# Curvature flow on one core: one clip for both curvatures, K added a period later, and GpSimd's second sum behind the addition of H

## The chip, the cores and the metric

The kernel runs on one core of a Trainium2 chip. The metric is the device time of one execution in microseconds, lower is better. Engines are named as in the profile: PE is TensorE, DVE is VectorE, ACT is ScalarE, POOL is GpSimd, SP is SyncE, which here only issues DMAs.

## What is computed

The input is 8 x 16 images of 512 x 512 floats. The first layer is ten steps of a curvature flow on each image, the second a pair of 3 x 3 convolutions over 16 channels with a residual. Per step (`_derivs` gives Sobel derivatives, each clipped to 10):

```python
ux, uy, uxx, uxy, uyy = _derivs(u)
g2 = ux * ux + uy * uy
denK = jnp.maximum(1.0 + g2, EPS)
K = jnp.clip((uxx * uyy - uxy * uxy) / (denK * denK + EPS), -5.0, 5.0)
denH = jnp.sqrt(1.0 + g2 + EPS)
H = ((1.0 + uy * uy) * uxx - 2.0 * ux * uy * uxy + (1.0 + ux * ux) * uyy) / (2.0 * denH ** 3 + EPS)
H = jnp.clip(H, -5.0, 5.0)
diff = jnp.clip(alpha * K + beta * H, -1.0, 1.0)
u = u + DT * diff
# then the border rows and columns are copied from their neighbours
```

After ten steps the layer gives `0.7 * u + 0.3 * x`; the convolutions follow.

## The kernel before

A short first stage scans the input and picks one of two versions of the flow. Here it picks the tame one (tiles named `tame_`), in which no field clip is needed and K and H are added to U directly. The last stage holds the two convolutions and is not touched.

The flow holds four images on the chip at once, U as 128 partitions x 2048 per image, worked on in halves ("chunks") of 128 x 1024. Every step of a chunk is one period of a software pipeline; 32 rounds x 10 steps x 8 chunks are 2560 periods. In period k each engine executes a fixed list, written out by hand in its own `period` function, which mixes chunk k with chunks k - 1 to k - 4. Engines wait for each other by semaphores, one per kind of operation, that count up by 2 for each chunk; `done(t, c)` is the count after chunk c. Since chunks k and k - 2 share buffers (`c % 2`), an operation on chunk k that writes a buffer waits for the last reader of chunk k - 2.

- PE (L646, L656): the derivatives `ux`, `uy` of chunk k (eight matmuls each), then for chunk k - 1 the subtraction of uxy squared from `ps["uxx"]` with a negative unit matrix, then `uyy`, `uxy`, `uxx` of k. `ux` waits for `term_uyy` of k - 1, `uy` for `term_uxy` of k - 1 (they share PSUM slots), `uyy` for `square_ux` and `uxy` for `square_uy` of k, `uxx` for `curvature_k` of k - 1.
- DVE: for k - 1 `term_uxx`, `term_uxy` (L517, into uy2 and cross), `determinant` (L540); for k - 2 `add_h` (L517, U from ux2); for k `multiply_first` (L536); in some periods `blend` (L517 into stage), the final 0.7/0.3 mix of a finished image; for k - 1 `curvature_k` (L559); for k `sum_squares` (L517 into slope); for k - 1 `curvature_h` (L570), `clip_k` (L565), `clip_h` (L575), `add_k` (L517, U from uyy); for k `term_uyy` (L517 into ux2).
- ACT: `power` (L441), `log_power` (L446) of k - 1, `copy_ux` (L397) of k, `inverse_k` (L436) of k - 1, `square_ux` (L402), `square_uy` (L408) of k, `inverse_h` (L452, into PSUM) of k - 1, `square_slope` (L426), `copy_uyy` (L414) of k, `high` (L391) of k - 4, `square_uxy` (L420) and `logs` (L431, both halves of slope) of k. In blend periods `scale` (L457) as well.
- POOL: `second_terms` (L362) and `numerator_h` (L368) of k - 1, both sums into ux2, then `low` (L356) of k - 4, the low part of U's split in two rounded parts.
- SP: the exchange of split halos (L281) in two halves, around `edge_columns` (L290), which waits for `updated`, and `edge_rows` (L298, L300).

`sum_squares` waits for `square_uy`, which waits for `multiply_first`. `curvature_h` waits for `numerator_h` and `inverse_h`. `high` waits for the border rows of its chunk, `low` for `high`. K lies in `uyy[c % 2]` and H in `ux2[c % 2]`, both in SBUF, as are U, slope, cross and stage; the derivatives and `inverse` lie in PSUM. The operations `blend` and `scale` occur in 8 periods of every round, 256 in all.

## Time and profile before

| | us |
|---|---|
| median of 3 runs | 38702.86 |
| the runs | 38694.59 to 38705.76 |
| the profiled execution | 38698.44 |
| its span | 38696.7 |
| DVE busy | 34434.0 |
| PE busy | 34434.2 |
| ACT busy | 33167.9 |
| POOL busy | 20465.8 |

The flow fills the span from about 412 to 35005 us; the scan is ahead of it, the convolutions behind. A busy time is the union of an engine's instructions. Instructions of one engine overlap a little in the records: the next starts slightly before the one ahead is noted as ended, so the distance from start to start is what an instruction costs its engine. "L517" is one helper line for all `scalar_tensor_tensor` operations; the tiles tell them apart.

### The profile page before, as it was taken

To read this page: it belongs to the slowest core of one execution; us is meant where nothing else is said; L and a number is where in the kernel's file an instruction comes from. 1 tells how busy PE (TensorE), PEld (TensorE's weight loads), DVE (VectorE), ACT (ScalarE), POOL (GpSimd) and SP (SyncE) were. 2 spreads that over 40 slices of the span, in tenths; PEclk is the share of its full clock that TensorE was granted. 3 is DMA by queue.
4 is the path that set the end of the run, shared out by engine and by line. 5 is a ranking of instruction groups with operands and counts; after the bars stand their busy time and mean duration, and the time that the engine had idled before them with its cause. 6 is when DMAs were issued, how large, how long until landed. Compare 5 with 4: busy or idle time off the path is not lost. (4 is left out here: it accounts for less than half of the span.)

```text
span 38696.7 us, 453600 instructions
## 1 busy us (share of the span) xinstructions
PE 34434.2 (89%) x126400; PEld 23294.9 (60%) x126400; DVE 34434.0 (89%) x33108; ACT 33167.9 (86%) x33722; POOL 20465.8 (53%) x7685
## 2 busy tenths in 40 slices
PE   5888888888888888888888888888888888889999
PEld 3666666666666666666666666666666666666666
DVE  8999999999999999999999999999999999993111
ACT  5999999999999999999999999999999999994333
POOL 3555555555555556555555555555555555550000
PEclk9999999999999999999999999999999999999999
DMA  5333333333333333333333333333333333333333
GB/s 189 83 83 82 82 75 78 83 83 82 82 83 83 82 79 74 81 83 83 83 82 83 83 83 76 77 81 83 83 83 82 83 83 80 73 82 83 87 87 85
DMA packets 2687511, 3261.71 MB, mean 84 GB/s; under 512 B 2266180, under 2 KB 2266308, under 8 KB 2364740
## 3 DMA queue, kind: packets, MB, share of 16 engines
q1 hardware_dynamic: 2686276, 3247.70, 33.5%
q8 instruction: 475, 7.78, 0.1%
q14 instruction: 760, 6.23, 0.0%
HBM read 582.33 MB, written 268.44 MB: 22 GB/s over the span
## 5 line engine op out<-in xcount | busy, mean ns | idle before, releaser
L646 PE MATMUL tame_slot<-tame_split,tame_M 128*128 128x512 f32 x51200 | 15156.1, 418 | 4131.5 <-DVE tame_ux L517 3386.6
L646 PEld LDWEIGHTS tame_slot<-tame_split,tame_M 128*128 128x128 f32 x51200 | 9160.8, 190 | 10140.8 <-issue 2690.5
L646 PE MATMUL tame_slot<-tame_halo,tame_M 128*128 128x512 f32 x51200 | 14319.2, 402 | 0.0
L356 POOL TENSOR_TENSOR tame_split<-tame_U,tame_split 128x1024 fp32r<-128x1024 f32 x2560 | 6232.0, 2434 | 12755.0 <-ACT tame_split L391 12755.0
L646 PEld LDWEIGHTS tame_slot<-tame_halo,tame_M 128*128 128x128 f32 x51200 | 9757.9, 191 | 2513.8
L368 POOL TENSOR_TENSOR tame_ux<-tame_ux,tame_cross 128x1024 f32<-128x1024 f32 x2560 | 8071.5, 3153 | 433.4 <-POOL tame_ux L362 433.4
L362 POOL TENSOR_TENSOR tame_ux<-tame_ux,tame_uy 128x1024 f32<-128x1024 f32 x2560 | 6161.8, 2407 | 972.6 <-DVE tame_uy L517 972.6
L431 ACT ACTIVATE tame_slope<-tame_slope 128x2048 f32<-128x2048 f32 x2560 | 4895.4, 1912 | 0.0
L656 PE MATMUL tame_slot<-tame_uxy,tame_unit 128*128 128x512 f32 x10240 | 4810.6, 592 | 5.4 <-DVE tame_slot L540 5.4
L426 ACT ACTIVATE tame_slope<-tame_slope 128x1024 f32<-128x1024 f32 x2560 | 2716.8, 1061 | 2141.4 <-issue 2139.4
L559 DVE TENSOR_TENSOR tame_uyy<-tame_slot,tame_slope 128x1024 f32<-128x1024 f32 x2560 | 3132.2, 1223 | 945.6 <-PE tame_slot L656 938.1
L517 DVE SCALAR_TENSOR_TENSOR tame_U<-tame_ux,tame_par,tame_U 128x1024 f32<-128x1024 f32 x2560 | 3694.1, 1443 | 0.1
L517 DVE SCALAR_TENSOR_TENSOR tame_U<-tame_uyy,tame_par,tame_U 128x1024 f32<-128x1024 f32 x2560 | 3272.3, 1278 | 0.0
L536 DVE TENSOR_TENSOR tame_cross<-tame_cross,tame_slot 128x1024 f32<-128x1024 f32 x2560 | 3093.9, 1209 | 158.5 <-PE tame_slot L646 157.2
L517 DVE SCALAR_TENSOR_TENSOR tame_uy<-tame_uy,tame_slot 128x1024 f32<-128x1024 f32 x2560 | 3106.9, 1214 | 27.0 <-issue 27.0
L540 DVE TENSOR_TENSOR tame_slot<-tame_uyy,tame_slot 128x1024 f32<-128x1024 f32 x2560 | 3127.3, 1222 | 0.0
L517 DVE SCALAR_TENSOR_TENSOR tame_slope<-tame_ux,tame_uy 128x1024 f32<-128x1024 f32 x2560 | 3110.9, 1215 | 1.8 <-ACT tame_uy L408 1.3
L517 DVE SCALAR_TENSOR_TENSOR tame_ux<-tame_ux,tame_slot 128x1024 f32<-128x1024 f32 x2560 | 3106.6, 1214 | 2.2 <-ACT tame_uyy L414 2.2
L570 DVE TENSOR_TENSOR tame_ux<-tame_ux,tame_slot 128x1024 f32<-128x1024 f32 x2560 | 3108.1, 1214 | 0.0
L517 DVE SCALAR_TENSOR_TENSOR tame_cross<-tame_cross,tame_slot 128x1024 f32<-128x1024 f32 x2560 | 3107.2, 1214 | 0.0
L862 DVE SCALAR_TENSOR_TENSOR res<-po,vec,xin 96x512 f32<-96x512 f32 x672 | 501.9, 747 | 2838.7 <-PE po L883 2838.7
L441 ACT ACTIVATE tame_slope<-tame_slope 128x1024 f32<-128x1024 f32 x2560 | 2718.2, 1062 | 234.9
(74 smaller groups left out, 38207.5 us busy)
## 6 DMA issues: line engine op xcount, KB each, us to landing
tame_halo<-tame_split SPq DMA_DIRECT2D x2560, 520.0 KB
tame_halo<-tame_split SPq DMA_DIRECT2D x2560, 260.0 KB
tame_halo<-tame_split SPq DMA_DIRECT2D x5120, 65.0 KB
tame_U<-in_x SPq DMA_DIRECT2D x256, 512.0 KB, 3.9
tame_stage<-in_x SPq DMA_DIRECT2D x128, 1024.0 KB, 4.9
mixed<-tame_stage SPq DMA_DIRECT2D x128, 1024.0 KB, 6.4
out<-res SPq DMA_DIRECT2D x672, 192.0 KB
xin<-mixed SPq DMA_DIRECT2D x344, 256.0 KB, 4.6
```

Source lines behind the costliest of these rows:

```text
L356: nc.gpsimd.tensor_tensor(split_rows(c, 1), half_rows(c), split_rows(c, 0).bitcast(F32), ALU.subtract).then_inc(lo_ready, 2)
L362: nc.gpsimd.tensor_tensor(ux2[c % 2][:, :], ux2[c % 2][:, :], uy2[c % 2][:, :], ALU.add).then_inc(sum_h, 2)
L368: nc.gpsimd.tensor_tensor(ux2[c % 2][:, :], ux2[c % 2][:, :], cross[c % 2][:, :], ALU.add).then_inc(num_h_ready, 2)
L431: nc.scalar.activation(both, both, ACT.Ln, bias=EPS).then_inc(logs_ready, 2)
L441: nc.scalar.activation(s, s, ACT.Exp, scale=1.5, bias=math.log(2.0)).then_inc(power_ready, 2)
L517: return nc.vector.scalar_tensor_tensor(out=out, in0=a, scalar=s, in1=b, op0=op0, op1=op1)
L536: nc.vector.tensor_tensor(cross[c % 2][:, :], cross[c % 2][:, :], ps["uy"][:, :], ALU.mult).then_inc(cross_ready, 2)
L540: nc.vector.tensor_tensor(ps["uxx"][:, :], uyy[c % 2][:, :], ps["uxx"][:, :], ALU.mult).then_inc(prod_k, 2)
L559: nc.vector.tensor_tensor(uyy[c % 2][:, :], ps["uxx"][:, :], slope[c % 2][:, 1, :], ALU.mult).then_inc(k_ready, 2)
L570: nc.vector.tensor_tensor(ux2[c % 2][:, :], ux2[c % 2][:, :], inverse[:, :], ALU.mult).then_inc(h_ready, 2)
L646: last = nc.tensor.matmul(ps[name][:, b * BANK:(b + 1) * BANK], M[0:lanes, matrix, :], rows(c, part)[:, b * y:(b + 1) * y, :], start=(n < ...
L656: last = nc.tensor.matmul(ps["uxx"][:, b * BANK:(b + 1) * BANK], unit[:, 0, :], uxy2[:, b * BANK:(b + 1) * BANK], start=False, stop=True, ...
```

## The change

K and H of a chunk now both lie in `slope[c % 2]`, K in half 1 and H in half 0, and a single instruction over both halves (128 x 2048), `clip_both`, takes the place of `clip_k` and `clip_h`. `add_k` moves from the end of the period of chunk k - 1 to just ahead of `add_h`, one period later. `uyy` becomes a single tile, and the waits on reuse follow the new owners of the buffers. `numerator_h` on GpSimd also waits for `updated` of the chunk before it, that is for `add_h` in the same period. ACT's order changes: `square_ux` behind `copy_ux`, then `inverse_k`, `inverse_h`, `scale`, `high`, then `square_uy`, `copy_uyy`, `square_slope`, `square_uxy`, `logs`.

```diff
--- before.py
+++ after.py
@@ -148,7 +148,8 @@
         def pair(name):
             return [sb(f"{name}{j}", [P, HALF]) for j in range(2)]
 
-        ux2, uy2, cross, uyy = pair("ux2"), pair("uy2"), pair("cross"), pair("uyy")
+        ux2, uy2, cross = pair("ux2"), pair("uy2"), pair("cross")
+        uyy = sb("uyy", [P, HALF])
         slope = [sb(f"slope{j}", [P, 2, HALF]) for j in range(2)]
         uxy2 = sb("uxy2", [P, HALF])
         par = sb("par", [P, 4])
@@ -194,9 +195,8 @@
         sum_h = sem("sum_h")
         num_h_ready = sem("num_h_ready")
         k_ready = sem("k_ready")
-        k_clipped = sem("k_clipped")
+        both_clipped = sem("both_clipped")
         h_ready = sem("h_ready")
-        h_clipped = sem("h_clipped")
         k_added = sem("k_added")
         diff_sum = sem("diff_sum")
         diff_clipped = sem("diff_clipped")
@@ -362,16 +362,18 @@
                 nc.gpsimd.tensor_tensor(ux2[c % 2][:, :], ux2[c % 2][:, :], uy2[c % 2][:, :],
                                         ALU.add).then_inc(sum_h, 2)
 
-            def numerator_h(t, c):
+            def numerator_h(t, c, after_update):
                 pool.wait_ge(cross_term, done(t, c))
                 pool.wait_ge(sum_h, done(t, c))
+                if after_update:
+                    pool.wait_ge(updated, done(t, c - 1))
                 nc.gpsimd.tensor_tensor(ux2[c % 2][:, :], ux2[c % 2][:, :], cross[c % 2][:, :],
                                         ALU.add).then_inc(num_h_ready, 2)
 
             def period(t, k, kind, r):
                 if exists(kind, k - 1):
                     second_terms(t, k - 1)
-                    numerator_h(t, k - 1)
+                    numerator_h(t, k - 1, exists(kind, k - 2))
                 if exists(kind, k - 4) and goes_on(kind, k - 4):
                     low(t, k - 4)
 
@@ -398,7 +400,7 @@
 
             def square_ux(t, c, fresh):
                 if not fresh:
-                    act.wait_ge(updated, done(t, c - 2))
+                    act.wait_ge(h_ready, done(t, c - 2))
                 nc.scalar.activation(ux2[c % 2][:, :], ps["ux"][:, :], ACT.Square).then_inc(ux2_ready, 2)
 
             def square_uy(t, c, fresh):
@@ -407,11 +409,11 @@
                     act.wait_ge(sum_h, done(t, c - 2))
                 nc.scalar.activation(uy2[c % 2][:, :], ps["uy"][:, :], ACT.Square).then_inc(uy2_ready, 2)
 
-            def copy_uyy(t, c, fresh):
+            def copy_uyy(t, c, first):
                 act.wait_ge(ready["uyy"], done(t, c))
-                if not fresh:
-                    act.wait_ge(k_added, done(t, c - 2))
-                nc.scalar.activation(uyy[c % 2][:, :], ps["uyy"][:, :], ACT.Copy).then_inc(uyy_copied, 2)
+                if not first:
+                    act.wait_ge(prod_k, done(t, c - 1))
+                nc.scalar.activation(uyy[:, :], ps["uyy"][:, :], ACT.Copy).then_inc(uyy_copied, 2)
 
             def square_uxy(t, c, first):
                 act.wait_ge(ready["uxy"], done(t, c))
@@ -422,7 +424,7 @@
             def square_slope(t, c, fresh):
                 act.wait_ge(slope_ready, done(t, c))
                 if not fresh:
-                    act.wait_ge(k_ready, done(t, c - 2))
+                    act.wait_ge(k_added, done(t, c - 2))
                 nc.scalar.activation(slope[c % 2][:, 1, :], slope[c % 2][:, 0, :], ACT.Square).then_inc(slope2_ready, 2)
 
             def logs(t, c):
@@ -471,21 +473,18 @@
                     log_power(t, k - 1)
                 if exists(kind, k):
                     copy_ux(t, k, fresh)
+                    square_ux(t, k, fresh)
+                if exists(kind, k - 1):
+                    inverse_k(t, k - 1)
+                    inverse_h(t, k - 1, kind == "first" and k == 1)
                 if exists(kind, k - 3) and ends(kind, k - 3):
                     scale(r, k - 3)
-                if exists(kind, k - 1):
-                    inverse_k(t, k - 1)
-                if exists(kind, k):
-                    square_ux(t, k, fresh)
-                    square_uy(t, k, fresh)
-                if exists(kind, k - 1):
-                    inverse_h(t, k - 1, kind == "first" and k == 1)
-                if exists(kind, k):
-                    square_slope(t, k, fresh)
-                    copy_uyy(t, k, fresh)
                 if exists(kind, k - 4) and goes_on(kind, k - 4):
                     next_high(t, k - 4, kind, r)
                 if exists(kind, k):
+                    square_uy(t, k, fresh)
+                    copy_uyy(t, k, first)
+                    square_slope(t, k, fresh)
                     square_uxy(t, k, first)
                     logs(t, k)
 
@@ -526,7 +525,7 @@
                 dve.wait_ge(ux2_ready, done(t, c))
                 dve.wait_ge(uy2_ready, done(t, c))
                 if not fresh:
-                    dve.wait_ge(inv_h_ready, done(t, c - 2))
+                    dve.wait_ge(updated, done(t, c - 2))
                 stt(slope[c % 2][:, 0, :], ux2[c % 2][:, :], 1.0, uy2[c % 2][:, :], ALU.add,
                     ALU.add).then_inc(slope_ready, 2)
 
@@ -537,7 +536,7 @@
                                         ALU.mult).then_inc(cross_ready, 2)
 
             def determinant(t, c):
-                nc.vector.tensor_tensor(ps["uxx"][:, :], uyy[c % 2][:, :], ps["uxx"][:, :], ALU.mult).then_inc(prod_k, 2)
+                nc.vector.tensor_tensor(ps["uxx"][:, :], uyy[:, :], ps["uxx"][:, :], ALU.mult).then_inc(prod_k, 2)
 
             def term_uyy(t, c):
                 dve.wait_ge(uyy_copied, done(t, c))
@@ -556,35 +555,32 @@
             def curvature_k(t, c):
                 dve.wait_ge(num_k_ready, done(t, c))
                 dve.wait_ge(inv_k_ready, done(t, c))
-                nc.vector.tensor_tensor(uyy[c % 2][:, :], ps["uxx"][:, :], slope[c % 2][:, 1, :],
-                                        ALU.mult).then_inc(k_ready, 2)
-
-            def clip_k(t, c):
-                K = uyy[c % 2][:, :]
-                dve.wait_ge(k_ready, done(t, c))
-                nc.vector.tensor_scalar(K, K, CURVATURE_CLIP, -CURVATURE_CLIP, ALU.min, ALU.max).then_inc(k_clipped, 2)
+                K = slope[c % 2][:, 1, :]
+                nc.vector.tensor_tensor(K, ps["uxx"][:, :], K, ALU.mult).then_inc(k_ready, 2)
 
             def curvature_h(t, c):
                 dve.wait_ge(num_h_ready, done(t, c))
                 dve.wait_ge(inv_h_ready, done(t, c))
-                nc.vector.tensor_tensor(ux2[c % 2][:, :], ux2[c % 2][:, :], inverse[:, :], ALU.mult).then_inc(h_ready, 2)
-
-            def clip_h(t, c):
-                Hh = ux2[c % 2][:, :]
+                nc.vector.tensor_tensor(slope[c % 2][:, 0, :], ux2[c % 2][:, :], inverse[:, :], ALU.mult).then_inc(
+                    h_ready, 2)
+
+            def clip_both(t, c):
+                both = slope[c % 2][:, :, :]
+                dve.wait_ge(k_ready, done(t, c))
                 dve.wait_ge(h_ready, done(t, c))
-                nc.vector.tensor_scalar(Hh, Hh, CURVATURE_CLIP, -CURVATURE_CLIP, ALU.min, ALU.max).then_inc(h_clipped, 2)
+                nc.vector.tensor_scalar(both, both, CURVATURE_CLIP, -CURVATURE_CLIP, ALU.min, ALU.max).then_inc(
+                    both_clipped, 2)
 
             def add_k(t, c):
-                K = uyy[c % 2][:, :]
-                dve.wait_ge(k_clipped, done(t, c))
+                K = slope[c % 2][:, 1, :]
+                dve.wait_ge(both_clipped, done(t, c))
                 if tame:
                     stt(half(c), K, a_dt, half(c), ALU.mult, ALU.add).then_inc(k_added, 2)
                 else:
                     nc.vector.tensor_scalar(K, K, a_dt, None, ALU.mult).then_inc(k_added, 2)
 
             def add_h(t, c):
-                K, Hh = uyy[c % 2][:, :], ux2[c % 2][:, :]
-                dve.wait_ge(h_clipped, done(t, c))
+                K, Hh = slope[c % 2][:, 1, :], slope[c % 2][:, 0, :]
                 dve.wait_ge(k_added, done(t, c))
                 if tame:
                     stt(half(c), Hh, b_dt, half(c), ALU.mult, ALU.add).then_inc(updated, 2)
@@ -607,6 +603,7 @@
                     term_uxy(t, k - 1)
                     determinant(t, k - 1)
                 if exists(kind, k - 2):
+                    add_k(t, k - 2)
                     add_h(t, k - 2)
                 if exists(kind, k):
                     clip("ux", t, k)
@@ -620,9 +617,7 @@
                     sum_squares(t, k, kind == "first" and k < 2)
                 if exists(kind, k - 1):
                     curvature_h(t, k - 1)
-                    clip_k(t, k - 1)
-                    clip_h(t, k - 1)
-                    add_k(t, k - 1)
+                    clip_both(t, k - 1)
                 if exists(kind, k):
                     clip("uyy", t, k)
                     term_uyy(t, k)
```

## Rows read from the trace of the kernel before

**Rows 1.** The page, part 1: busy time of each engine, its share, instructions.

```profile
PE 34434.2 (89%) x126400; PEld 23294.9 (60%) x126400; DVE 34434.0 (89%) x33108; ACT 33167.9 (86%) x33722; POOL 20465.8 (53%) x7685
```

**Rows 2.** Timeline, VectorE, a steady period: start, duration, engine, line, out<-in [idle before].

```profile
5011.40 1.22 DVE L517 SCALAR_TENSOR_TENSOR tame_uy<-tame_uy,tame_slot 128x1024 f32<-128x1024 f32 x1
5012.53 1.22 DVE L517 SCALAR_TENSOR_TENSOR tame_cross<-tame_cross,tame_slot 128x1024 f32<-128x1024 f32 x1
...
5014.80 1.44 DVE L517 SCALAR_TENSOR_TENSOR tame_U<-tame_ux,tame_par,tame_U 128x1024 f32<-128x1024 f32 x1
5016.16 1.21 DVE L536 TENSOR_TENSOR tame_cross<-tame_cross,tame_slot 128x1024 f32<-128x1024 f32 x1
5017.77 1.23 DVE L559 TENSOR_TENSOR tame_uyy<-tame_slot,tame_slope 128x1024 f32<-128x1024 f32 x1 [0.40 <-PE tame_slot L656]
5018.91 1.22 DVE L517 SCALAR_TENSOR_TENSOR tame_slope<-tame_ux,tame_uy 128x1024 f32<-128x1024 f32 x1
5020.05 1.22 DVE L570 TENSOR_TENSOR tame_ux<-tame_ux,tame_slot 128x1024 f32<-128x1024 f32 x1
...
5021.78 0.69 DVE L575 TENSOR_SCALAR tame_ux<-tame_ux 128x1024 f32<-128x1024 f32 x1
5022.38 1.28 DVE L517 SCALAR_TENSOR_TENSOR tame_U<-tame_uyy,tame_par,tame_U 128x1024 f32<-128x1024 f32 x1
5023.58 1.21 DVE L517 SCALAR_TENSOR_TENSOR tame_ux<-tame_ux,tame_slot 128x1024 f32<-128x1024 f32 x1
5024.71 1.22 DVE L517 SCALAR_TENSOR_TENSOR tame_uy<-tame_uy,tame_slot 128x1024 f32<-128x1024 f32 x1
```

**Rows 3.** Timeline, ScalarE, the same period and the next.

```profile
5010.63 1.92 ACT L431 ACTIVATE tame_slope<-tame_slope 128x2048 f32<-128x2048 f32 x1
5012.64 1.06 ACT L441 ACTIVATE tame_slope<-tame_slope 128x1024 f32<-128x1024 f32 x1
...
5020.21 1.06 ACT L426 ACTIVATE tame_slope<-tame_slope 128x1024 f32<-128x1024 f32 x1 [0.75 <-issue]
...
5030.81 1.03 ACT L408 ACTIVATE tame_uy<-tame_slot 128x1024 f32<-128x1024 f32 x1
```

**Rows 4.** Instructions on U: duration min/median/max in ns, first and last start, form.

```profile
L356 POOL TENSOR_TENSOR tame_split<-tame_U,tame_split x2560: 2167/2438/2460, 388.8 to 34924.8; 128x1024 fp32r<-128x1024 f32 x197
L517 DVE SCALAR_TENSOR_TENSOR tame_U<-tame_uyy,tame_par,tame_U x2560: 1269/1278/1284, 433.1 to 34997.8; 128x1024 f32<-128x1024 f32 x197
L517 DVE SCALAR_TENSOR_TENSOR tame_U<-tame_ux,tame_par,tame_U x2560: 1285/1444/1457, 438.8 to 34999.2; 128x1024 f32<-128x1024 f32 x197
...
L517 DVE SCALAR_TENSOR_TENSOR tame_stage<-tame_U,tame_stage x256: 1216/2249/3361, 1413.4 to 35004.8; 128x1024 f32<-128x1024 f32 x128
```

**Rows 5.** Timeline, GpSimd, the same steady period.

```profile
5012.75 2.40 POOL L362 TENSOR_TENSOR tame_ux<-tame_ux,tame_uy 128x1024 f32<-128x1024 f32 x1 [0.34 <-DVE tame_uy L517]
5015.32 3.15 POOL L368 TENSOR_TENSOR tame_ux<-tame_ux,tame_cross 128x1024 f32<-128x1024 f32 x1 [0.17 <-POOL tame_ux L362]
```

**Rows 6.** Timeline, GpSimd, the program's first period.

```profile
425.92 2.38 POOL L368 TENSOR_TENSOR tame_ux<-tame_ux,tame_cross 128x1024 f32<-128x1024 f32 x1 [0.17 <-POOL tame_ux L362]
```

**Rows 7.** Timeline, all engines, two periods with a blend (L517 into tame_stage).

```profile
1476.96 1.21 DVE L517 SCALAR_TENSOR_TENSOR tame_slope<-tame_ux,tame_uy 128x1024 f32<-128x1024 f32 x1
...
1486.67 3.14 POOL L368 TENSOR_TENSOR tame_ux<-tame_ux,tame_cross 128x1024 f32<-128x1024 f32 x1 [0.17 <-POOL tame_ux L362]
...
1488.64 2.25 DVE L517 SCALAR_TENSOR_TENSOR tame_stage<-tame_U,tame_stage 128x1024 f32<-128x1024 f32 x1
...
1491.95 1.21 DVE L517 SCALAR_TENSOR_TENSOR tame_slope<-tame_ux,tame_uy 128x1024 f32<-128x1024 f32 x1
...
1497.88 1.83 PE L646 MATMUL tame_slot<-tame_split,tame_M 128*128 128x512 f32 x4 [1.95 <-DVE tame_ux L517]
```

**Rows 8.** Timeline, TensorE, the steady period: second derivative, then the subtraction.

```profile
5013.81 1.22 PE L646 MATMUL tame_slot<-tame_split,tame_M 128*128 128x512 f32 x4
...
5015.80 1.88 PE L656 MATMUL tame_slot<-tame_uxy,tame_unit 128*128 128x512 f32 x4
```

## The prediction

> **What bounds the kernel now.** I read the page's first part, then a timeline of one steady period, engine by engine, then durations by tile, then a stretch with the blend. The page has PE and DVE both busy 89% of the span and ACT 86% [rows 1]; none is plainly the bound, so the period must be walked. On DVE (DVE names VectorE, ACT ScalarE, PE TensorE, POOL GpSimd) the period runs from `term_uxx` at 5011.40 to the next at 5024.71: 13.31 us [rows 2]. A tensor operation with two inputs holds its place for 1.13 to 1.14 us, a clip for 0.60, `add_k` for 1.20, and `add_h` for 1.36. There is one idle gap, before `curvature_k`, ended by PE's subtraction (0.40 noted; the start comes 1.61 after `multiply_first` where 1.13 would do, so 0.48). Without it DVE's work is 12.83.
>
> ACT is nearly as tight. From `sum_squares` (5018.91) to `square_slope` is 1.30, from there to the next `square_uy` 10.60 with no gap, its 1.03 and a signal of 0.11 (between the 0.09 from PE to `curvature_k` and the 0.13 from DVE to POOL [rows 2, 5, 8]) release the next `sum_squares`: 13.04 around [rows 2, 3]. So no rearrangement that keeps this loop wins more than 0.27 us a period.
>
> The rows of most weight are those where DVE and POOL meet. `add_h` (inputs U and the H tile, both in SBUF) takes 1.44, but 1.285 at its shortest [rows 4]; it starts 0.35 before `second_terms` ends on POOL, and loses 0.16 [rows 2, 5]. POOL's `numerator_h`, started 0.92 before `add_h` ends, takes 3.15; in the very first period, with no `add_h` beside it, 2.38 [rows 5, 6]: it loses 0.77. The blend, again two SBUF inputs, starts at 1488.64 under a POOL operation that ends at 1489.81, and takes 2.25 in place of 1.22; the longest blend took 3.36 [rows 4, 7]. If it streams for its last 1.22 us, it got going 0.14 before POOL ended. Meanwhile `multiply_first` and `curvature_k`, with one PSUM input, take their 1.21 and 1.23 under the same POOL operation [rows 2, 5]. I read this as: a DVE operation that needs both of its SBUF inputs and a POOL operation take turns, whole instruction by whole instruction, first come first.
>
> **The change, part by part.** There are 2560 periods (one for every `add_k` [rows 4]); 256 hold a blend, 2304 don't. I set zero at the start of `sum_squares` in the new order.
>
> *Clips.* Two of 0.60 become one over 2048 elements. A pitch of 0.60 is 0.07 besides 0.53 for 1024 elements (two-input operations: 0.07 and 1.07), so the double one is 1.14: gain 0.06. But it now directly follows `curvature_h`, on which it waits, where `clip_k` stood between. A dependent operation can't start 0.08 before the end of the one ahead, as DVE's others do. ACT's `power` shows a dependent start 0.09 after the end (5010.63 + 1.92 to 5012.64, [rows 3]). For DVE I take 0.06, between 0 and 0.10: `curvature_h` holds its place for 1.28 instead of 1.13. Cost 0.15 (0.08 to 0.19).
>
> *`add_k` moved.* It comes right in front of `add_h`, which waits for it: again 0.15 (0.08 to 0.19). And it falls where `add_h` falls today: 3.40 after `term_uxx`, while `second_terms` on POOL, started 1.35 after `term_uxx`, runs to 3.75 [rows 2, 5]. So it pays the 0.16 that `add_h` pays: 1.50 in all.
>
> *The wait on POOL.* `numerator_h` starts only once `add_h` has ended, so neither blocks the other: `add_h` holds 1.20, and POOL's operation takes 2.38. Gain for DVE 0.16. Who waits for it: `curvature_h`, later by four DVE operations, and `low` queued behind it on POOL; see below.
>
> *DVE's sum, nothing yet in its way:* `sum_squares` 1.13, `curvature_h` 1.28, `clip_both` 1.14, `term_uyy` 1.13, `term_uxx` 1.13, `term_uxy` 1.14, `determinant` 1.13, `add_k` 1.50, `add_h` 1.20, `multiply_first` 1.13, `curvature_k` 1.13: 13.04.
>
> *PE.* The unit subtraction begins 1.99 after `uy` begins and takes 1.88; `curvature_k` starts 3.96 after `uy`'s start, which follows `term_uxy`'s start by 1.28 [rows 2, 8]: 5.24. Today only 4.76 of DVE work lies between, hence the gap of 0.48. The new order has `add_k` in there as well: 1.14 + 1.13 + 1.50 + 1.20 + 1.13 = 6.10. The gap vanishes.
>
> *ACT reordered.* `square_ux` and `high` come earlier, `copy_uyy` now follows `square_uy`. The same operations stand between `square_slope` and `square_uy`, save that `inverse_h` replaces `copy_uyy`: 13.04 within 0.05. But `multiply_first` now comes late: start to end 1.21, signal 0.10, `square_uy` 1.03, signal 0.11: `sum_squares` follows it by 2.45, DVE's own order by 2.26. That is 0.19 of new waiting: 13.23. The new conditions on `slope`, `ux2` and the single `uyy` tile name operations half a period old or more; I cost them at nothing. The SP queue keeps its order: `edge_columns` waits for `updated`, which comes 2.4 ahead of `sum_squares` (2.67 now), and the first half of the exchange can start earlier, as `low` does.
>
> *`low`, the expensive part.* `add_h` ends at -2.37 (0.08 after `multiply_first` starts). POOL begins `numerator_h` 0.13 later (as 5012.62 to 5012.75 [rows 2, 5]) and ends at +0.14. `high` has been done since about -1.0, so `low` starts at once. `sum_squares`, two SBUF inputs, already runs since 0; `low` waits until it ends at 1.22. As a POOL operation then needs what `numerator_h` needed after `add_h`, its base (2.17 for `low` [rows 4]) less about 0.15, `low` ends near 3.24. `clip_both` wants to start at 2.41. If it takes turns with POOL too, it gets going 0.14 before that end, at 3.10: 0.69 lost. No POOL operation meets a clip today, so the bounds are 0 and 2.17. I take the 0.69, since the nearest rows speak for it: a clip does 1024 elements in 0.69 where others need 1.22 [rows 2], two at a time, SBUF to SBUF, so it needs as much of SBUF as a two-input operation.
>
> The Trainium skill says the same of both kinds: "GPSIMD Engine Reference", section "Key points", has contention with DVE instructions in a 2-port perf mode or with two SBUF inputs. Of the second kind [rows 4 to 7] agree; of the first no row here shows anything. By this rule the loss is the 0.69, without it the sum would stay at 13.23.
>
> Period: 13.23 + 0.69 = 13.92; I round to 13.88, as 0.14 may be 0.19 by `add_h`'s own row (5015.15 less 5014.96). Against 13.31: +0.57 x 2304 = +1313.
>
> *Blend periods.* Today 14.99 from `sum_squares` to `sum_squares` [rows 7]. New: the blend follows `multiply_first` while POOL runs `numerator_h`; it gets going 0.14 before that ends, at 2.37 after `add_h`'s end, and ends at 3.59. `low` waits for it and ends at 3.59 + 2.02 = 5.61. `sum_squares` could start at 4.64 but gets going at 5.47, in place of 2.37; `clip_both` is then free (less 0.69). 13.92 + 3.10 - 0.69 = 16.33, +1.3 x 256 = +333. PE then idles longer ahead of `ux` than the 1.95 after which a half derivative took 1.83 instead of 1.22 [rows 7, 8], the granted clock at the lower of its levels; up to 1.4 a period, at most 360, only in the range.
>
> Sum: +1646 on the profiled execution's 38698.4 (its span of 38696.7 and 1.7 around it; 4 under the median of the runs, 38702.9): 40,344.
>
> **Rivals.**
> A. *The clip doesn't take turns with POOL.* For: no row shows that it does. Against: its speed. Steady period 13.19, -0.12 x 2304 = -276, blend +333: +57, 38,760. Chance 0.11.
> B. *Faster: `low` is out of the clip's way*, because POOL isn't held by `sum_squares` when it comes second, or finishes before 2.41. `low` would run from 0.14 to 2.3, and the blend periods cost what they cost now. This decides if `low` ends under 2.41. With short signals the period falls toward the 13.04 of ACT's loop: -0.12 to -0.27, centre -0.2 x 2560 = -510: 38,190. Against: `numerator_h` was held 0.77 by `add_h` in just this way. Chance 0.15.
> C. *`low` gets in ahead of `sum_squares`.* It starts 0.14 behind it, so a signal or two decides. Then `sum_squares` loses some 2.0 and the clip nothing: 13.23 + 2.0 = 15.2, +1.9 x 2304 + 333 = +4700: 43,400. Against: the order of starts holds itself up, both hang on `add_h`. Chance 0.05.
> D. *Dependent DVE starts cost nothing.* "VectorE: DVE Perf Modes", section "The DRAIN you can't avoid", has a semaphore between copies cost nothing extra. By that the two terms of 0.15 go: -0.30 x 2560 = -768. As a mechanism of this kernel, priced from rows: DVE operations start 0.08 before the end of the one ahead [rows 2], and a dependent one would too; 40,344 - 768 = 39,580. ACT's 0.09 after the end speaks against it. Chance 0.07.
>
> **How the numbers follow.** Forecast 0.62, own range 39,900 to 40,750; A 0.11, B 0.15, C 0.05, D 0.07. The range from 38,500 to 40,800 leaves out C and most of B. Under 0.2% (77 us) a measurement tells nothing from no change. Slower: forecast, C, D and a fourth of A, 0.77; same: most of A, 0.08; faster: B, 0.15.
>
> **What would show it.** Right: one clip of 128x2048, over 1.7 on average against 1.2 uncontended; `low` near 3.0 instead of 2.44; `numerator_h` near 2.4; `add_k` 1.44 and `add_h` 1.28; no idle before `curvature_k` by PE; `sum_squares` idle about 0.2 behind ACT. Wrong: a clip of 1.2 with `low` beside it (A); `low` at 2.2 to 2.4 (B); `sum_squares` over 3 (C); the start of `add_h` before the end of `add_k` (D); a clip of 2.2 with nothing beside it, which would mean one element at a time and near +1.1 a period without my 0.69.

## The result and the profile after

The changed kernel takes 41,177.5 us (median of 4 runs, 41,160.7 to 41,304.3) against 38,698.7 before: a ratio of 1.065, with a 95% interval of 1.063 to 1.067. (A ratio is a kernel's time over that of the kernel before; its interval stands behind it.) It is slower, as forecast, but by 2479 us where 1646 were forecast, and outside the range. The profiled execution took 41,304.3 (span 41,302.5), the longest of the four, 2606 over the one of before.

The page of the changed kernel, part 1 and three groups of part 5 (busy us, mean ns | idle before, releaser); the first row answers to [rows 1]:

```profile
PE 34840.2 (84%) x126400; PEld 23669.3 (57%) x126400; DVE 36722.5 (89%) x30548; ACT 33735.5 (82%) x33722; POOL 20031.4 (48%) x7685
...
L370 POOL TENSOR_TENSOR tame_ux<-tame_ux,tame_cross 128x1024 f32<-128x1024 f32 x2560 | 6143.0, 2400 | 6779.9 <-DVE tame_U L516 6779.7
L356 POOL TENSOR_TENSOR tame_split<-tame_U,tame_split 128x1024 fp32r<-128x1024 f32 x2560 | 7849.8, 3066 | 142.7 <-ACT tame_split L393 140.8
...
L571 DVE TENSOR_SCALAR tame_slope<-tame_slope 128x2048 f32<-128x2048 f32 x2560 | 4492.4, 1755 | 346.5
```

DVE is busier by 2289 us with fewer instructions; `numerator_h` (L370) fell to its 2.4, `low` (L356) rose from 2.43 to 3.07, and the one clip (L571) takes 1.76 on average where the two took 1.37 together.

A steady period, all engines, in order of time; it answers to [rows 2, 3, 5]:

```profile
2015.07 1.23 DVE L516 SCALAR_TENSOR_TENSOR tame_slope<-tame_ux,tame_uy 128x1024 f32<-128x1024 f32 x1 [0.18 <-ACT tame_uy L410]
2015.16 3.23 POOL L356 TENSOR_TENSOR tame_split<-tame_U,tame_split 128x1024 fp32r<-128x1024 f32 x1
...
2016.21 1.21 DVE L564 TENSOR_TENSOR tame_slope<-tame_ux,tame_slot 128x1024 f32<-128x1024 f32 x1
...
2017.56 1.90 DVE L571 TENSOR_SCALAR tame_slope<-tame_slope 128x2048 f32<-128x2048 f32 x1
...
2019.38 1.21 DVE L516 SCALAR_TENSOR_TENSOR tame_ux<-tame_ux,tame_slot 128x1024 f32<-128x1024 f32 x1
...
2020.51 1.21 DVE L516 SCALAR_TENSOR_TENSOR tame_uy<-tame_uy,tame_slot 128x1024 f32<-128x1024 f32 x1
...
2021.86 2.40 POOL L362 TENSOR_TENSOR tame_ux<-tame_ux,tame_uy 128x1024 f32<-128x1024 f32 x1 [3.47 <-DVE tame_uy L516]
2022.78 1.22 DVE L539 TENSOR_TENSOR tame_slot<-tame_uyy,tame_slot 128x1024 f32<-128x1024 f32 x1
...
2023.91 2.83 DVE L516 SCALAR_TENSOR_TENSOR tame_U<-tame_slope,tame_par,tame_U 128x1024 f32<-128x1024 f32 x2
...
2026.65 1.21 DVE L535 TENSOR_TENSOR tame_cross<-tame_cross,tame_slot 128x1024 f32<-128x1024 f32 x1
...
2026.88 2.41 POOL L370 TENSOR_TENSOR tame_ux<-tame_ux,tame_cross 128x1024 f32<-128x1024 f32 x1 [2.63 <-DVE tame_U L516]
...
2027.79 1.22 DVE L559 TENSOR_TENSOR tame_slope<-tame_slot,tame_slope 128x1024 f32<-128x1024 f32 x1
2027.95 1.03 ACT L410 ACTIVATE tame_uy<-tame_slot 128x1024 f32<-128x1024 f32 x1
...
2029.18 1.23 DVE L516 SCALAR_TENSOR_TENSOR tame_slope<-tame_ux,tame_uy 128x1024 f32<-128x1024 f32 x1 [0.18 <-ACT tame_uy L410]
```

From `sum_squares` to `sum_squares` it is 14.11. `low` starts 0.09 behind `sum_squares` and takes 3.23; the clip starts 2.49 after `sum_squares` and takes 1.90. `numerator_h` starts 0.23 after `multiply_first` does and is done in 2.41, `add_k` and `add_h` together take 2.83, and there is no gap ahead of `curvature_k` now.

Minimum, median and maximum of two operations on slope, in ns:

```profile
L516 DVE SCALAR_TENSOR_TENSOR tame_slope<-tame_ux,tame_uy x2560: 1206/1225/3292, 419.3 to 37586.9; 128x1024 f32<-128x1024 f32 x197
...
L571 DVE TENSOR_SCALAR tame_slope<-tame_slope x2560: 1226/1891/1910, 433.9 to 37602.6; 128x2048 f32<-128x2048 f32 x197
```

So the clip takes 1.226 at its shortest: it runs at two elements at a time, and what it takes beyond that is waiting. `sum_squares` reaches 3.29; before it never took more than 1.23.

Taking all starts of `sum_squares` in this trace: of 2306 plain periods (periods without a blend) 1847 take 14.1 or 14.2 us, and nearly all the others are longer; together they lie 424 us above 14.11. Of the 456 that are over by more than 0.13 (called long below), 392 have the lower clock in them or in the period ahead. The periods with a blend take 16.62 on average, against 15.04 before. Here is what a long plain one looks like:

```profile
2219.82 1.92 PE L641 MATMUL tame_slot<-tame_split,tame_M 128*128 128x512 f32 x4 [1.75 <-DVE tame_ux L516]
...
2221.53 1.91 PE L641 MATMUL tame_slot<-tame_halo,tame_M 128*128 128x512 f32 x4
...
2223.53 1.03 ACT L399 ACTIVATE tame_cross<-tame_slot 128x1024 f32<-128x1024 f32 x1 [1.99 <-PE tame_slot L641]
...
2228.46 2.21 POOL L356 TENSOR_TENSOR tame_split<-tame_U,tame_split 128x1024 fp32r<-128x1024 f32 x1
...
2229.43 2.31 DVE L516 SCALAR_TENSOR_TENSOR tame_slope<-tame_ux,tame_uy 128x1024 f32<-128x1024 f32 x1 [1.03 <-ACT tame_uy L410]
...
2233.01 1.23 DVE L571 TENSOR_SCALAR tame_slope<-tame_slope 128x2048 f32<-128x2048 f32 x1
```

PE idled 1.75 ahead of `ux`. The two halves of `ux` then take 1.92 and 1.91 in place of the 1.19 and 1.11 that they take in the steady period above (from 2020.74): the granted clock was at the lower of its two levels. `copy_ux` sits idle 1.99 behind it, all of ACT's list is late, and `low` gets in at 2228.46, 0.97 ahead of `sum_squares`, which now takes 2.31, while the clip is free at 1.23. The period in which the clock falls takes 15.27, the next 14.53.

And two periods with a blend, to be read beside [rows 7]. In the first PE had its full clock from one `sum_squares` to the next, in the second it had not:

```profile
4991.78 2.39 POOL L370 TENSOR_TENSOR tame_ux<-tame_ux,tame_cross 128x1024 f32<-128x1024 f32 x1 [2.65 <-DVE tame_U L516]
...
4992.69 2.56 DVE L516 SCALAR_TENSOR_TENSOR tame_stage<-tame_U,tame_stage 128x1024 f32<-128x1024 f32 x1
...
4994.13 3.20 POOL L356 TENSOR_TENSOR tame_split<-tame_U,tame_split 128x1024 fp32r<-128x1024 f32 x1
...
4996.31 2.09 DVE L516 SCALAR_TENSOR_TENSOR tame_slope<-tame_ux,tame_uy 128x1024 f32<-128x1024 f32 x1
...
5009.48 1.06 ACT L459 ACTIVATE tame_stage<-tame_stage 128x1024 f32<-128x1024 f32 x1
...
5010.57 1.24 DVE L516 SCALAR_TENSOR_TENSOR tame_stage<-tame_U,tame_stage 128x1024 f32<-128x1024 f32 x1 [1.28 <-ACT tame_stage L459]
```

In the first the blend waits for nothing and takes 2.56: `numerator_h` on POOL holds it. `low` gets its turn behind the blend, ahead of `sum_squares`, which takes 2.09. In the second ACT is late by the low clock, and the blend waits 1.28 for `scale`, which ACT's new order put behind `inverse_h`. That wait occurs in 168 of the 256 blends, nearly always behind a stretch at the low clock. The period comes out the same: 16.61 on average where the blend does not wait and 16.63 where it does.

### The profile page after: what moved, and what is told of

The parts are those of the page before. It is cut to its first block and busy times, and to the rows that moved or that the text cites. A ratio compares the mean times of both kernels' runs of the same rounds, so it can differ in the third digit from the quotient of the medians.

```text
span 41302.5 us, 451326 instructions
## 1 busy us (share of the span) xinstructions
PE 34840.2 (84%) x126400; PEld 23669.3 (57%) x126400; DVE 36722.5 (89%) x30548; ACT 33735.5 (82%) x33722; POOL 20031.4 (48%) x7685
## 5 line engine op out<-in xcount | busy, mean ns | idle before, releaser
L641 PE MATMUL tame_slot<-tame_split,tame_M 128*128 128x512 f32 x51200 | 16386.4, 443 | 6329.9 <-DVE tame_ux L516 4795.2
L370 POOL TENSOR_TENSOR tame_ux<-tame_ux,tame_cross 128x1024 f32<-128x1024 f32 x2560 | 6143.0, 2400 | 6779.9 <-DVE tame_U L516 6779.7
L356 POOL TENSOR_TENSOR tame_split<-tame_U,tame_split 128x1024 fp32r<-128x1024 f32 x2560 | 7849.8, 3066 | 142.7 <-ACT tame_split L393 140.8
L516 DVE SCALAR_TENSOR_TENSOR tame_U<-tame_slope,tame_par,tame_U 128x1024 f32<-128x1024 f32 x5120 | 6966.0, 1361 | 293.7
L571 DVE TENSOR_SCALAR tame_slope<-tame_slope 128x2048 f32<-128x2048 f32 x2560 | 4492.4, 1755 | 346.5
L428 ACT ACTIVATE tame_slope<-tame_slope 128x1024 f32<-128x1024 f32 x2560 | 2719.1, 1062 | 2270.1 <-issue 1914.6
L399 ACT ACTIVATE tame_cross<-tame_slot 128x1024 f32<-128x1024 f32 x2560 | 2627.2, 1026 | 1383.2 <-PE tame_slot L641 1382.7
L559 DVE TENSOR_TENSOR tame_slope<-tame_slot,tame_slope 128x1024 f32<-128x1024 f32 x2560 | 3114.2, 1216 | 54.4 <-PE tame_slot L651 40.2
L564 DVE TENSOR_TENSOR tame_slope<-tame_ux,tame_slot 128x1024 f32<-128x1024 f32 x2560 | 3103.1, 1212 | 1.0 <-POOL tame_ux L370 1.0
L410 ACT ACTIVATE tame_uy<-tame_slot 128x1024 f32<-128x1024 f32 x2560 | 2625.4, 1026 | 512.8 <-issue 480.8
```

The lines of the kernel that those rows point to most:

```text
L356: nc.gpsimd.tensor_tensor(split_rows(c, 1), half_rows(c), split_rows(c, 0).bitcast(F32), ALU.subtract).then_inc(lo_ready, 2)
L370: nc.gpsimd.tensor_tensor(ux2[c % 2][:, :], ux2[c % 2][:, :], cross[c % 2][:, :], ALU.add).then_inc(num_h_ready, 2)
L516: return nc.vector.scalar_tensor_tensor(out=out, in0=a, scalar=s, in1=b, op0=op0, op1=op1)
L559: nc.vector.tensor_tensor(K, ps["uxx"][:, :], K, ALU.mult).then_inc(k_ready, 2)
L564: nc.vector.tensor_tensor(slope[c % 2][:, 0, :], ux2[c % 2][:, :], inverse[:, :], ALU.mult).then_inc(h_ready, 2)
L571: nc.vector.tensor_scalar(both, both, CURVATURE_CLIP, -CURVATURE_CLIP, ALU.min, ALU.max).then_inc(both_clipped, 2)
```

## The experiments

**e1: GpSimd without its new wait.**

```diff
-                if after_update:
-                    pool.wait_ge(updated, done(t, c - 1))
```

> The changed kernel without GpSimd's new wait. Theory (DVE operations with two SBUF inputs and POOL operations take turns whole): numerator_h gets its turn when add_k ends, add_h waits for it, 2.23 less 0.14, about 2.0 later; low is then out of the clip's way (0.67 back). Steady period 14.11 + 1.3 = 15.4, kernel near 44,000 us; add_h over 3 us, the clip 1.23. Rival (the wait itself is what costs, since it delays numerator_h and low): the period falls to about 13.4 and the kernel to 39,500.

Measured: 45,102 us, ratio 1.166 (1.164 to 1.168). Its timeline, DVE's pair of additions and `numerator_h`, then `term_uxx` of a later period:

```profile
2004.72 4.76 DVE L514 SCALAR_TENSOR_TENSOR tame_U<-tame_slope,tame_par,tame_U 128x1024 f32<-128x1024 f32 x2
...
2005.25 3.15 POOL L368 TENSOR_TENSOR tame_ux<-tame_ux,tame_cross 128x1024 f32<-128x1024 f32 x1 [0.17 <-POOL tame_ux L362]
...
2017.48 1.22 DVE L514 SCALAR_TENSOR_TENSOR tame_uy<-tame_uy,tame_slot 128x1024 f32<-128x1024 f32 x1 [0.70 <-PE tame_slot L639]
```

The pair takes 4.76 instead of 2.83, 1.93 more: `numerator_h` got its turn between the two and `add_h` waited it out. Periods are 15.4 where the clock holds, as expected, but more than half are 16.1. All but one of these have the lower clock in them (0.934 over the span), and `term_uxx` waits 0.70 for PE's `uxx`. The wait on POOL isn't what costs; without it the changed kernel is slower by 3900 us, some 1100 of them by these longer periods.

**e2: the clip behind `term_uyy`.**

```diff
                 if exists(kind, k - 1):
                     curvature_h(t, k - 1)
-                    clip_both(t, k - 1)
                 if exists(kind, k):
                     clip("uyy", t, k)
                     term_uyy(t, k)
+                if exists(kind, k - 1):
+                    clip_both(t, k - 1)
+                if exists(kind, k):
```

> The changed kernel with clip_both behind term_uyy instead of ahead of it. Theory: the clip starts 3.4 after sum_squares, when low has just ended (3.2), so it isn't held (0.67 back), and nothing on DVE waits for the instruction right ahead of it there (0.2 back): period 14.11 - 0.87 = 13.24, or up to 13.4 where ACT's loop binds; kernel 39,100 to 39,500. Rival (the clip's hold is hidden, ACT or PE sets the period): no more than 0.1 a period, kernel above 40,900.

Measured: 38,852 us, ratio 1.004 (1.003 to 1.006); 2326 under the changed kernel, and 250 under the low end of what was expected. Its timeline, `low`, `term_uyy` and the clip:

```profile
2004.11 3.23 POOL L356 TENSOR_TENSOR tame_split<-tame_U,tame_split 128x1024 fp32r<-128x1024 f32 x1
...
2006.30 1.21 DVE L516 SCALAR_TENSOR_TENSOR tame_ux<-tame_ux,tame_slot 128x1024 f32<-128x1024 f32 x1
...
2007.43 1.22 DVE L571 TENSOR_SCALAR tame_slope<-tame_slope 128x2048 f32<-128x2048 f32 x1
```

`low` ends at 2007.34 and the clip starts at 2007.43: not held, 1.22. The steady period is 13.20. The granted clock is back at 0.992 and far fewer plain periods are long (127 in place of 456); `term_uyy` now releases `ux` earlier, and PE idles 1.12 ahead of `uy` in place of 1.73 ahead of `ux`. That is the part that I hadn't counted. Blend periods stay at 16.33. The plain period is thus below the 13.31 of the kernel before; the blend periods (15.04 before) cost more than that wins.

**e3: a small `low`** (2 of a chunk's 16 rows; the other low parts are left out).

```diff
-                nc.gpsimd.tensor_tensor(split_rows(c, 1), half_rows(c), split_rows(c, 0).bitcast(F32),
+                nc.gpsimd.tensor_tensor(split_rows(c, 1)[:, 0:2, :], half_rows(c)[:, 0:2, :],
+                                        split_rows(c, 0)[:, 0:2, :].bitcast(F32),
```

> The changed kernel with GpSimd's low computed for 2 of a chunk's 16 rows only; the rest of the low parts is left out. Theory: low is done well before the clip: clip 1.23, period 14.11 - 0.67 = 13.44, blend periods lose their hold on sum_squares (0.8 back), kernel about 39,300. Rival (the clip takes 1.9 for another reason, its shape for instance): clip still 1.9, kernel within 200 us of the changed one.

Measured: 39,181 us, ratio 1.013 (1.011 to 1.014). The clip's row among the operations on slope:

```profile
L572 DVE TENSOR_SCALAR tame_slope<-tame_slope x2560: 1226/1227/1230, 436.2 to 35482.5; 128x2048 f32<-128x2048 f32 x197
```

It is 1.227 at the median and 1.230 at most: with the same shape in the same place, the clip waits for nothing once `low` is gone. The period is 13.45. That is the price of the meeting: 0.66 a period. The changed kernel's own trace has it too: its three periods from 431 to 472 us, ahead of the pipeline's first `low`, take 13.45. Of the 1997 us between the two kernels the meeting itself is 0.66 x 2304 = 1520, the blend periods (15.69 in place of 16.62) are 240; the other 240 or so are long periods, which are nearly gone with it (67 are left; granted clock 0.994; PE idles 1.05 ahead of `ux` in place of 1.73).

**e4: `high`, and `low` behind it, moved back.**

```diff
-                if exists(kind, k - 4) and goes_on(kind, k - 4):
-                    next_high(t, k - 4, kind, r)
                 if exists(kind, k):
                     square_uy(t, k, fresh)
                     copy_uyy(t, k, first)
                     square_slope(t, k, fresh)
+                if exists(kind, k - 4) and goes_on(kind, k - 4):
+                    next_high(t, k - 4, kind, r)
+                if exists(kind, k):
                     square_uxy(t, k, first)
```

> The changed kernel with high (and so low behind it) put behind square_slope in ACT's order, nearer to where it stood before. Theory: low then starts about 3.5 after sum_squares, when the clip (2.5 to 3.7) has its turn already, and ends before second_terms starts: clip 1.23, low near 2.4, steady period 14.11 - 0.67 = 13.44, blend periods about 15.7 since low no longer gets ahead of sum_squares; kernel near 39,200. Rival (the reordering of ACT isn't what brings low onto the clip, or a later high delays square_uxy and logs by as much): period above 13.9, kernel above 40,500.

Measured: 39,180 us, ratio 1.012 (1.011 to 1.014), the time of e3 with all the work done. The clip and `low`:

```profile
2012.84 1.23 DVE L572 TENSOR_SCALAR tame_slope<-tame_slope 128x2048 f32<-128x2048 f32 x1
...
2013.81 2.30 POOL L356 TENSOR_TENSOR tame_split<-tame_U,tame_split 128x1024 fp32r<-128x1024 f32 x1 [3.35 <-ACT tame_split L393]
```

The clip comes first, and `low` is held by it for a tenth or two only. The period is 13.45, blend periods 15.69. So it is the reordering on ACT, `high` put ahead of `square_uy`, that brought `low` onto the clip. What is left of the change still costs 480 us: 13.45 in place of 13.31 in plain periods, 15.69 in place of 15.04 in those with a blend.

**e5: PE fed.**

```diff
+                if name == "uxx":
+                    for _ in range(6):
+                        nc.tensor.matmul(ps[name][:, 0:BANK], M[0:P, f, :], split_rows(c, 0)[:, 0:BANK // PX, :],
+                                         start=True, stop=True)
```

> The changed kernel with six more matmuls at the start of each uxx (they are overwritten by the real ones), which fill most of PE's idle time of 1.7 ahead of ux. Theory: the periods of 14.5 to 15.3 come from a granted clock that falls after that idle time; fed, they go: steady period 14.11 everywhere, granted clock 0.99 or more, kernel 150 to 400 us faster than the changed one. Rival (they come from DMA or from the order of waits): the same number of long periods and no gain, or slower by the added work.

Measured: 41,021 us, 156 under the changed kernel, with more work (ratio 1.060, 1.058 to 1.062). The same stretch of 800 us, between two runs of blends, in this kernel and in the changed one (busy time and instructions of PE, weight loads, DVE, ACT, POOL; granted clock, DMA share, GB/s):

```profile
1600.00:2400.00 800.00, 758.68 (x2822) 520.88 (x2821) 775.13 (x622) 712.85 (x679) 449.11 (x171) 1.00 0.29 70
```

```profile
1600.00:2400.00 800.00, 678.69 (x2468) 459.24 (x2466) 771.57 (x618) 707.04 (x674) 440.34 (x169) 0.99 0.29 70
```

The granted clock is 1.00 instead of 0.99 there, 0.996 instead of 0.979 over the span. The steady period is 14.14 (0.03 more, some 80 us), and 162 of the plain periods are long in place of 456, only ten of them at or right behind a stretch at the lower clock; so the falls of the clock cost the changed kernel some 240 us in its median run. The theory holds; the size was at the low end of what was expected.

**e6: the wait alone, on the kernel before.** The four lines of the change's `numerator_h` and its call, nothing else.

> The kernel before with nothing but GpSimd's new wait (numerator_h behind add_h). Theory: add_h falls to 1.28 and numerator_h to 2.4, but DVE's gap ahead of curvature_k grows from 0.40 to 0.56, since PE's chain from term_uxy (5.24) sets that start: steady period 13.31 as before, blend periods longer by up to 0.3; kernel 38,700 to 38,790. Rival (what add_h saves is kept): 0.16 x 2560 = 410 us faster, 38,290.

Measured: 38,764 us, ratio 1.0015 (1.0006 to 1.0024). `add_h` and `curvature_k`:

```profile
2001.66 1.44 DVE L519 SCALAR_TENSOR_TENSOR tame_U<-tame_ux,tame_par,tame_U 128x1024 f32<-128x1024 f32 x1
...
2004.64 1.22 DVE L561 TENSOR_TENSOR tame_uyy<-tame_slot,tame_slope 128x1024 f32<-128x1024 f32 x1 [0.41 <-PE tame_slot L658]
```

The time is as expected, one of the reasons isn't: `add_h` still takes 1.44. What holds it is the end of `second_terms`, not `numerator_h`, as [rows 2, 5] would have told me. Blend periods rose from 15.04 to 15.30, and that is the 60 us. There was nothing to gain from this wait before `add_k` moved.

**e7: two clips in the place of one.**

```diff
-                both = slope[c % 2][:, :, :]
+                K, Hh = slope[c % 2][:, 1, :], slope[c % 2][:, 0, :]
                 dve.wait_ge(k_ready, done(t, c))
+                nc.vector.tensor_scalar(K, K, CURVATURE_CLIP, -CURVATURE_CLIP, ALU.min, ALU.max).then_inc(
+                    both_clipped, 1)
                 dve.wait_ge(h_ready, done(t, c))
-                nc.vector.tensor_scalar(both, both, CURVATURE_CLIP, -CURVATURE_CLIP, ALU.min, ALU.max).then_inc(
-                    both_clipped, 2)
+                nc.vector.tensor_scalar(Hh, Hh, CURVATURE_CLIP, -CURVATURE_CLIP, ALU.min, ALU.max).then_inc(
+                    both_clipped, 1)
```

> The changed kernel with clip_both as two clips again, K's first, in the same place. Theory: clip_k needn't wait for curvature_h and would start 0.2 earlier, but is held until low is 0.14 from its end all the same; the two then cost 1.20 instead of 1.15: steady period 14.11 to 14.2, kernel within 200 us of the changed one. Rival (the double clip or its wait on curvature_h is the cost): period 0.2 to 0.7 shorter, kernel under 40,700.

Measured: 42,173 us, ratio 1.090: a miss by 800. The shortest periods are 14.18, as expected, and the first clip takes 1.58, the second 0.68. But in a stretch of 138 plain periods only some 60 are that short. PE's `ux`, `low` and `sum_squares` in one that isn't:

```profile
2000.46 1.20 PE L643 MATMUL tame_slot<-tame_split,tame_M 128*128 128x512 f32 x4 [1.80 <-DVE tame_ux L516]
...
2009.03 2.21 POOL L356 TENSOR_TENSOR tame_split<-tame_U,tame_split 128x1024 fp32r<-128x1024 f32 x1
2009.23 3.10 DVE L516 SCALAR_TENSOR_TENSOR tame_slope<-tame_ux,tame_uy 128x1024 f32<-128x1024 f32 x1 [0.16 <-ACT tame_uy L410]
```

PE idled 1.80 this time, and the clock fell in the middle of `ux` (granted clock 0.954 over the span). With a period 0.07 longer the lower clock fills 3.9 ms of the span in place of 1.7.

**e9: e7 with e5's matmuls.**

> e7_two_clips with the six overwritten matmuls of e5_pe_fed. Theory: the 1000 us that e7_two_clips lost beyond the changed kernel are periods after a fall of the granted clock (0.954 there), since PE's idle time ahead of ux is 1.8 instead of 1.7; fed, only the steady 14.18 is left: granted clock 0.99 or more, kernel 41,000 to 41,250, near e5_pe_fed's 41,021. Rival (the two clips themselves cost it): above 41,900.

Measured: 41,059 us, ratio 1.061 (1.060 to 1.063), granted clock 0.996, periods of 14.18. The 1000 us were the clock, and the two clips themselves cost 40 us beside e5. Where PE is fed, joining the clips is worth next to nothing, since a hold by `low` ends both ways at the same moment; in the changed kernel it is worth 996 us (e7), nearly all by way of the clock.

**e11: `add_k` back at its old time**, right behind the clip.

```diff
                 if exists(kind, k - 2):
-                    add_k(t, k - 2)
                     add_h(t, k - 2)
...
                     clip_both(t, k - 1)
+                    add_k(t, k - 1)
```

> The changed kernel with add_k back at its old time, now right behind clip_both, and the rest as changed. Theory: moving it was worth nothing by itself: it waits for the clip in place of add_h waiting for it, and add_h meets second_terms in its place (0.16): steady period 14.1 to 14.2 apart from the clock. PE idles 1.2 longer ahead of ux, so more periods follow a fall of the granted clock: kernel 41,300 to 43,000. Rival (the later addition is what made the period 0.8 longer): period near 13.4, kernel under 40,000.

Measured: 47,838 us, ratio 1.236 (granted clock 0.906): a miss by 4800, on the side that I had named. PE's `ux`, `copy_ux`, `multiply_first`, `low` and `sum_squares`:

```profile
2001.83 2.04 PE L641 MATMUL tame_slot<-tame_split,tame_M 128*128 128x512 f32 x4 [3.55 <-DVE tame_ux L516]
...
2003.67 1.78 PE L641 MATMUL tame_slot<-tame_halo,tame_M 128*128 128x512 f32 x4
...
2005.55 1.03 ACT L399 ACTIVATE tame_cross<-tame_slot 128x1024 f32<-128x1024 f32 x1 [2.73 <-PE tame_slot L641]
...
2007.50 1.22 DVE L535 TENSOR_TENSOR tame_cross<-tame_cross,tame_slot 128x1024 f32<-128x1024 f32 x1 [1.09 <-PE tame_slot L641]
...
2010.47 2.21 POOL L356 TENSOR_TENSOR tame_split<-tame_U,tame_split 128x1024 fp32r<-128x1024 f32 x1 [1.50 <-ACT tame_split L393]
...
2011.43 2.32 DVE L516 SCALAR_TENSOR_TENSOR tame_slope<-tame_ux,tame_uy 128x1024 f32<-128x1024 f32 x1 [1.03 <-ACT tame_uy L410]
```

Here nearly every period is a long one, 17.05 (`sum_squares` is held in 2552 of 2560). PE idles 3.55 ahead of `ux`, `ux` then takes 3.6 at the low clock, `copy_ux` waits 2.73 for it, `multiply_first` 1.09 for `uy`, `square_uy` is late, `low` gets in first and holds `sum_squares` for another 1.1, and all that leaves PE idle again. So the addition of K moved a period later is no loss by itself: with the other parts as they are, it spares PE this idle time. That the low clock keeps this going is read from the trace alone: no run feeds PE here. The expected 14.1 to 14.2 apart from the clock can't be read, since after the first few periods (13.69 to 14.48) hardly one keeps the clock.

**e8: e2 with the blend moved** between `add_k` and `add_h`, and `scale` ahead of `copy_ux` (the diff shows the blend's new place only).

```diff
                 if exists(kind, k - 2):
                     add_k(t, k - 2)
+                if exists(kind, k - 3) and ends(kind, k - 3):
+                    blend(t, k - 3, r)
+                if exists(kind, k - 2):
                     add_h(t, k - 2)
```

> e2_clip_later with the blend put between add_k and add_h, where POOL is idle, and ACT's scale ahead of copy_ux. Theory: the blend periods of 16.3 are long since the blend is held by numerator_h (1.1) and in turn lets low in ahead of sum_squares (0.8); in the new place nothing holds it and it also covers the wait of add_h on add_k: 13.2 + 1.1 = 14.3, so 2.0 x 256 = 510 us less than e2_clip_later: 38,340, 0.9% faster than before. Rival (the blend then waits for border rows or for scale, or ACT's loop binds): half of that or less, 38,600 or more.

Measured: 38,449 us, ratio 0.9934 (0.9921 to 0.9948): 0.7% faster than the kernel before, 403 under e2 where 510 were expected. DVE in a period with a blend (the first row is `add_k`, the last `add_h`):

```profile
1446.11 1.43 DVE L516 SCALAR_TENSOR_TENSOR tame_U<-tame_slope,tame_par,tame_U 128x1024 f32<-128x1024 f32 x1
...
1447.46 1.21 DVE L516 SCALAR_TENSOR_TENSOR tame_stage<-tame_U,tame_stage 128x1024 f32<-128x1024 f32 x1
...
1448.60 1.27 DVE L516 SCALAR_TENSOR_TENSOR tame_U<-tame_slope,tame_par,tame_U 128x1024 f32<-128x1024 f32 x1
```

The blend takes 1.21, held by nothing, and the period is 14.13 instead of 16.33 at the median. But 85 of the blend periods take more than 14.5, up to 16.2, and the average is 14.57; that is what is missing from the 510. What makes these long was not settled.

**e10: e8 with e5's matmuls.**

> e8_blend_moved with the six overwritten matmuls. Theory: its few long periods (one of 15.1 ahead of and one of 15.5 in each run of blends, and some of 15 elsewhere) also come from the clock: 1 to 3 us a round in each, 32 rounds, so 50 to 200 us faster than e8_blend_moved, 38,250 to 38,400, granted clock 0.995 or more. Rival (PE's added 1.4 us a period are on the path now that the period is 13.2): slower than e8_blend_moved.

Measured: 40,608 us, ratio 1.050: the rival was right. The six matmuls (in 1.61) and `term_uxx`:

```profile
2018.85 1.61 PE L642 MATMUL tame_slot<-tame_split,tame_M 128*128 128x512 f32 x6
...
2022.47 1.22 DVE L516 SCALAR_TENSOR_TENSOR tame_uy<-tame_uy,tame_slot 128x1024 f32<-128x1024 f32 x1 [0.86 <-PE tame_slot L648]
```

`term_uxx` sits idle 0.86 behind PE's `uxx`, and the period is 14.13. Filling PE pays where PE has room before the next reader, as in e5; here 0.93 of the added 1.4 us went onto the path. The granted clock is 0.998, and 126 plain periods are still longer than the rest (94 in e8), so the clock does not explain all of those either. Whether fewer matmuls would have gained was not tried.

## Why the prediction was wrong, step by step

- **What bounds the kernel, and that instructions take turns.** Right. A DVE operation with two SBUF inputs and a POOL operation exclude each other whole (e1: `add_h` held until `numerator_h` ends), and the clip, with one input at two elements at a time, is held too: 1.89 against 1.23 (e3). For this kind the trace of before had no row; the Trainium skill ("GPSIMD Engine Reference", "Key points": contention with DVE instructions in a 2-port perf mode or with two SBUF inputs) had it right for both; the price of the second is 0.66 to 0.67 us here against my 0.69. (That two elements at a time are the page's 2-port mode is read from the clip's speed.) So rival A falls, and rival B with it: `low` ends 3.3 after the start of `sum_squares`, not under 2.41.
- **Rival D** falls: with a wait on the instruction right ahead, the clip starts 1.35 after `curvature_h`, 0.14 after its end, and so it does in e3, where nothing holds it. The same clip in e2, behind an operation that it doesn't wait for, starts 1.13 after it. The Trainium skill ("VectorE: DVE Perf Modes", "The DRAIN you can't avoid") measured that a semaphore after each of eight copies cost nothing extra; here the wait costs 0.22, and the measurement decides.
- **The terms of the steady period, 13.88 forecast and 14.11 measured.** The step that failed here is the size of three terms, each in the right direction: up to the clip's start 2.49 instead of 2.41, the two additions 2.74 from start to start instead of 2.70, `multiply_first` to `sum_squares` 2.53 instead of 2.45. The rest (1.82 instead of 1.83 for the clip, 4.53 for four operations) was right. I took DVE's own signal as 0.06 where the trace shows 0.14 ahead of the clip and 0.12 between the additions, and the signal from ACT to DVE as 0.11 where it is 0.20 (`square_uy` ends at 2028.98, `sum_squares` starts at 2029.18); and I rounded 13.92 down on top. 0.23 x 2304 = 530 us, the largest part of the miss. It alone puts the time above the range.
- **The blend periods, 16.33 forecast and 16.62 measured.** Right in kind: the blend is held by `numerator_h`, `low` gets in front of `sum_squares`, and the clip is free. About 0.2 of the 0.29 are the undersized terms again, which stand in these periods too. The wait for `scale`, which I hadn't followed, comes with the low clock and leaves the period as it is. 75 us.
- **PE's clock.** This is the step that failed in kind: a cost put at nothing. I saw that PE would idle longer in the blend periods and kept 360 us for that in the range, at nothing in the sum. But DVE's later `term_uyy` makes PE idle 1.66 to 1.75 ahead of `ux` in every period (1.21 to 1.31 before), and now and then the clock falls. The fall then costs twice, by rival C's mechanism: ACT comes late and `low` gets in front of `sum_squares`. Some 360 us in the profiled execution, 240 in the median run (e5). The long idle time was itself a consequence of the clip's hold: with `low` out of its way PE idles 1.05 and most of the long periods go (e3, e4). I gave rival C 0.05 as a steady state, and didn't think of it as what one late period sets off: in 273 plain periods `sum_squares` is held over 0.3 us by a `low` ahead of it.
- **The wait on POOL and the move of `add_k`.** Right as a pair (e1: 3900 us worse without the wait), wrong in my reckoning of each alone. I had the wait gain DVE 0.16; on the kernel before it gains nothing (e6), since `second_terms` is what holds `add_h`. I priced the move at a loss of 0.31 (0.15 for the dependence, 0.16 for the meeting with `second_terms`) and never asked what its absence does to PE (e11).
- Together: 530 + 75 + 240 = 845; the miss is 2479 - 1646 = 833. That it comes out so close is in part luck, since each of the three is an estimate to some tens of us.

## What to carry to other kernels

When an edit moves an instruction that needs both of VectorE's SBUF inputs, or that runs at two elements at a time, lay GpSimd's whole list beside VectorE's, and price every meeting at what is left of the one that started first. Moving it one place past an operation that reads PSUM can be worth the whole meeting, and the wait on its neighbour too (e2: 2326 us, of which 0.66 a period for the meeting and 0.25 more with the wait gone). And when the period is walked, note for TensorE not only when it is needed but how long it idles: a kernel that has it idle a little longer may pay by a lower granted clock, and a single late period can reverse an order of turns that holds otherwise.

## What was not expected of the hardware

- The granted clock depends on little: idle times of 1.21 to 1.31 ahead of `ux` went with 0.992 over the span, 1.66 to 1.75 with 0.979, 1.80 with 0.954, 3.5 with 0.906, and the fed kernel with 0.996. These kernels differ in other idle times too: e1 has 0.934, though PE idles ahead of `ux` in under half of its periods there (1.06 at the median); it idles 2.25 behind `square_uy` in nearly all. So the idle time ahead of `ux` alone doesn't decide it, and the runs don't show a limit.
- The fall seems able to keep itself up: in e11 nearly every period shows it, 17.05 us each. That is argued from the trace; no run of e11 with PE fed exists.
- A POOL operation queued behind another with nothing to wait for starts a little before the end noted for the one ahead: in the steady period above `numerator_h` ends at 2029.29 and the next `low` starts at 2029.24. DVE can still come between: `sum_squares` starts at 2029.18, 0.11 ahead of that noted end, isn't held (1.23), and `low` waits for it (3.25). In e7 above, `low` starts 0.20 ahead of `sum_squares`, and `sum_squares` takes 3.10.
